# Moving the last exchange's four unchanged blocks, three roundings, the weights' means and one context low part in a gated cross-attention and ternary feed-forward kernel

## Time and profile before

| | |
|---|---|
| median of 3 runs | 649.63 us (649.16 to 651.08) |
| the profiled execution | 650.32 us, its span 648.5 us |
| VectorE, ScalarE, GpSimd busy | 534.8, 422.4, 359.5 us (82%, 65%, 55%) |
| granted TensorE clock | full in all 40 slices |
| chain that ended last | TensorE 75%, VectorE 13%, SyncE's queue 3% |
| DMA | 112.79 MB, mean 174 GB/s |

### The profile page before, as it was taken

One profiled execution on the slowest core, in us unless ns is written; L12 is line 12 of the kernel. 1 busy time (PEld: TensorE's weight loads), 2 busy tenths in 40 slices (PEclk: granted clock), 3 DMA queues, 4 the chain that ended last, 5 costly groups with the idle time before them and its releaser, 6 DMA issues.

```text
span 648.5 us, 9998 instructions
## 1 busy us (share of the span) xinstructions
PE 634.8 (98%) x2968; PEld 394.7 (61%) x2968; DVE 534.8 (82%) x869; ACT 422.4 (65%) x694; POOL 359.5 (55%) x304
## 2 busy tenths in 40 slices
PE   8799999999999999999999999999999999999997
PEld 7565566666666666666666756675656554544553
DVE  5778887789778887878789978897899987998863
ACT  2575686477647765775567766776666632688875
POOL 4712477556635653565367864664457145686651
PEclk9999999999999999999999999999999999999999
DMA  8207985799589948984888789868789881000001
GB/s 292 81 6 202 295 213 118 209 248 258 116 218 271 236 112 244 261 224 108 242 228 223 202 227 249 224 190 205 190 220 254 202 207 45 1 4 31 16 35 49
DMA packets 45208, 112.79 MB, mean 174 GB/s; under 512 B 11888, under 2 KB 15088, under 8 KB 45040
## 3 DMA queue, kind: packets, MB, share of 16 engines
q1 hardware_dynamic: 41648, 102.93, 59.3%
q10 hardware_dynamic: 3456, 9.37, 4.8%
q0 software_dynamic: 64, 0.00, 0.0%
HBM read 45.16 MB, written 2.10 MB: 73 GB/s over the span
## 4 chain that ended last, share of the span: by engine, by line
PE 75%; DVE 13%; SPq 3%; issue 3%; ACT 3%; POOL 1%; DMA 1%; POOLq 0%; DVEq 0%; ACTq 0%
PE ps_s L1462 13%; PE ps_ctx L1494 6%; PE ps_b L1494 6%; PE ps_s L624 5%; PE ps_b L1358 4%; PE ps_b L1413 4%; PE ps_b L1360 3%; PE ps_b L1359 3%; PE ps_b L1432 3%; SPq L1144 3%; DVE small L1884 3%; DVE E L1898 2%; PE ps_b L675 2%; PE ps_b L1490 2%; PE ps_ctx L1490 2%
## 5 line engine op out<-in xcount | busy, mean ns | idle before, releaser
L1260 POOL TENSOR_TENSOR G_lo<-G,g_hi 128x512 fp32r<-128x512 f32 x130 | 167.7, 1303 | 115.5 <-ACT g_hi L1638 115.5
L1696 ACT ACTIVATE E<-ps_s,small 128x1024 f32<-128x1024 f32 x128 | 142.3, 1114 | 133.3 <-DVE small L1884 110.5
L1884 DVE TENSOR_REDUCE small<-ps_s 128x1 f32<-128x1024 f32 x128 | 149.8, 1210 | 37.2 <-PE ps_s L1462 37.0
L1898 DVE STREAM_TRANSPOSE E<-E 128x1024 f32<-128x1024 f32 x124 | 151.9, 1229 | 0.1
L1218 POOL TENSOR_SCALAR E<-E,small 128x1024 f32<-128x1024 f32 x64 | 78.6, 1228 | 107.0 <-DVE small L1890 95.3
L1638 ACT ACTIVATE g_hi<-G 128x512 fp32r<-128x512 f32 x130 | 77.1, 630 | 3.5 <-DVE wq L1914 3.5
L1358 PE MATMUL ps_b<-b_hi,ctx_hi 128*128 128x512 f32 x128 | 66.8, 522 | 0.5 <-DVE ctx_lo L1844 0.5
L1494 PE MATMUL ps_ctx<-G,kv 128*128 128x512 f32 x126 | 64.6, 607 | 0.1
L1494 PE MATMUL ps_b<-G,kv 128*128 128x512 f32 x126 | 63.7, 600 | 0.8 <-DMA G<-E 0.8
L1462 PE MATMUL ps_s<-k_hi,q_hi 64*128 64x512 f32 x256 | 57.3, 444 | 3.6 <-ACT E L1696 3.4
L624 PE MATMUL ps_s<-wq,q12T 128*128 128x512 fp8e4 x256 | 59.8, 379 | 0.1
(11 more groups left out here) (202 smaller groups left out, 1210.7 us busy)
## 6 DMA issues: line engine op xcount, KB each, us to landing
G<-E SPq DMA_DIRECT2D x486, 128.0 KB, 3.0
w_stage<-in_wffn SPq DMA_DIRECT2D x37, 512.0 KB, 5.0
w_stage<-in_wffn ACTq DMA_DIRECT2D x11, 512.0 KB, 4.5
wo_s<-in_woT SPq DMA_DIRECT2D x8, 512.0 KB, 5.3
wq_s<-in_wq SPq DMA_DIRECT2D x7, 512.0 KB, 5.6
wkcq_s<-in_wkcqT SPq DMA_DIRECT2D x7, 384.0 KB, 3.3
out<-x_sb SPq DMA_DIRECT2D x8, 256.0 KB, 2.0
x_sb<-in_x SPq DMA_DIRECT2D x3, 512.0 KB, 7.0
```

What stands on the lines that cost most here:

```text
L1260: nc.gpsimd.tensor_tensor(g_tile(w % 2, i, G_lo), tile, high_part(i).bitcast(F32).rearrange("p (t i q) -> p t i q", t=ST, i=4), ALU.subtra ...
L1696: nc.scalar.activation(out, scores, ACT.Exp, bias=negmax[:, k:k + 1], accum_out=rowsum[:, k:k + 1]).then_inc(exp_done, 1)
L1884: nc.vector.tensor_reduce(negmax[:, k:k + 1], ps_s[:, t % 2, :], AX_X, ALU.max, negate=True).then_inc(max_done, 1)
L1898: nc.vector.transpose(e_tile(w % 2, t), e_tile(w % 2, t)).then_inc(blocks_turned, 1)
```

## The change

- **Exchange of (7,3).** Four of its 16 blocks, those that stay on their partitions, are no longer DMAs: GpSimd copies (0,0) and (2,2) (`keep_pool`), ScalarE (1,1) and (3,3) (`keep_act`), 32 partitions by 1024 elements each. SyncE issues the other twelve; ScalarE issues none. TensorE's first product of (7,3) waits for the twelve and for both engines' copies. GpSimd's copies stand before `ln2_root(0)` and between it and `rms_root(0)`. SyncE's load of g3 waits for the twelve as well.
- **Rounding.** In (5,0), (6,0) and (6,3) the first of the two roundings moves from before the third transpose to between the two maxima of the unit three ahead.
- **Means.** The mean product moves from before pair 4 to behind its first side task "m", VectorE's four operations into the first unit of pair 4 behind the context's low part. The wait on `mean_chain` stays for pair 4 alone.
- **Context's low part.** That of (7,2) moves from the start of (7,3) to step 6 of (7,2), behind the second row tile's quantised rows and before three small steps.

```diff
-SHARED = {(0, 1): 12, (7, 3): 10}
+SHARED = {(0, 1): 12}
+KEPT_POOL, KEPT_ACT = (0, 1), (2, 3)
+KEPT = len(KEPT_POOL) + len(KEPT_ACT)
...
+LATE_ROUND_STEPS, LATE_ROUNDS = (5, 6), ((5, 0), (6, 0), (6, 3))
...
+        CTX_LOW_AT = (2, 6)
...
             sp.wait_ge(exchanged[0], EXCHANGE * UNITS // 2)
+            sp.wait_ge(exchanged[1], exchanged_by(PAIRS - 1, 3))
             sp.dma_start(g3, A["g3"].partition_broadcast(P)).then_inc(ld_g3, 16)
...
                 norm_quant(dve, *ROWQUANT_AT[at])
+            if at == CTX_LOW_AT:
+                ctx_low(dve, PAIRS - 1, 2)
             if at in ROWDEQ_AT:
...
-            move_blocks(sp, w, BLOCKS[0:SHARED.get((p, w), len(BLOCKS))] if isinstance(p, int) else BLOCKS)
+            if isinstance(p, int) and (p, w) == (PAIRS - 1, 3):
+                move_blocks(sp, w, BLOCKS[KEPT:])
+            else:
+                move_blocks(sp, w, BLOCKS[0:SHARED.get((p, w), len(BLOCKS))] if isinstance(p, int) else BLOCKS)
...
             act.wait_ge(blocks_turned, 16 * p + (4 * w + 4))
-            if not (is0(p) and w < 2):
-                act.wait_ge(pv_done, 4 * p + (w - 1))
             move_blocks(act, w, BLOCKS[lo:hi])
+        def kept_block(i):
+            quarter = slice(BLOCKS[i][0] * QUAD, (BLOCKS[i][0] + 1) * QUAD)
+            return G[quarter, 1, BLOCKS[i][0], :, :], E[quarter, 1, BLOCKS[i][0], :, :]
+        def exchanged_by(p, w):
+            kept = 16 * KEPT if isinstance(p, int) and (p, w) == (PAIRS - 1, 3) else 0
+            return 2 * EXCHANGE * p + (EXCHANGE * (w // 2 + 1) - kept)
...
+        def keep_pool(pool, i, of, done):
+            pool.wait_ge(of, done)
+            pool.wait_ge(blocks_turned, 16 * PAIRS)
+            pool.wait_ge(pv_done, UNITS - 2)
+            into, rows = kept_block(KEPT_POOL[i])
+            nc.gpsimd.tensor_copy(into, rows).then_inc(kept_pool, 1)
+            pool.wait_ge(kept_pool, i + 1)
...
+                if last and w == 2:
+                    keep_pool(pool, 0, atanh_pool, 5)
                 if splits(p, w):
                     split_low(pool, p, w, 0)
...
                 if last and w == 2:
+                    keep_pool(pool, 1, ln2_done, 1)
                     rms_root(pool, 0)
...
-                pe.wait_ge(exchanged[w % 2], 2 * EXCHANGE * p + EXCHANGE * (w // 2 + 1))
+                pe.wait_ge(exchanged[w % 2], exchanged_by(p, w))
+                if isinstance(p, int) and (p, w) == (PAIRS - 1, 3):
+                    pe.wait_ge(kept_pool, len(KEPT_POOL))
+                    pe.wait_ge(kept_act, len(KEPT_ACT))
...
+                    if mean and (w, c) == (0, 0):
+                        mean_matmul(pe)
...
-            mean_matmul(pe)
             for p in range(4, 7):
-                pe_pair(pe, p, "mid", mean=True)
+                pe_pair(pe, p, "mid", mean=p == 4)
...
+        def keep_act(act, i):
+            act.wait_ge(blocks_turned, 16 * PAIRS)
+            act.wait_ge(pv_done, UNITS - 2)
+            into, of = kept_block(i)
+            copy_act(into, of).then_inc(kept_act, 1)
...
                     if variant == "last" and (w, c) == (2, 0):
-                        exchange_rest(act, 7, 3, 10, 13)
+                        keep_act(act, KEPT_ACT[0])
                     if variant == "last":
                         ffn_act_early(act, w, c)
                     if variant == "last" and (w, c) == (2, 1):
-                        exchange_rest(act, 7, 3, 13, 16)
+                        keep_act(act, KEPT_ACT[1])
...
+        def weight_means(dve):
+            dve.wait_ge(w_total, 1)
...
+            nc.vector.reciprocal(w_inv, w_eps).then_inc(mean_chain, 1)
...
+                late = isinstance(p, int) and (p, w) in LATE_ROUNDS
                 def rounded(c):
...
-                            if c == ROUND_STEPS[i]:
+                            if c == (LATE_ROUND_STEPS if late else ROUND_STEPS)[i]:
                                 round_half(dve, q, g)
...
-                if w or variant != "first":
+                if (w or variant != "first") and not (variant == "last" and w == 3):
                     ctx_low(dve, *((p, w - 1) if w else (p - 1, 3)))
+                if isinstance(p, int) and (p, w) == (SUM_PAIRS, 0):
+                    weight_means(dve)
...
                 if first:
                     max_tile(dve, *u3, 0)
+                    rounded(5)
                     max_tile(dve, *u3, 1)
```

More of the change, by code:

```diff
@@ L373, in build @@
         exchanged = [sem("exchanged0"), sem("exchanged1")]
+        kept_pool, kept_act = sem("kept_pool"), sem("kept_act")
         first_turned, first_act = (sem(n) for n in ("first_turned", "first_act"))
@@ L1915, in round_half @@
                                     MAGIC, MAGIC, ALU.add, ALU.subtract, saturate=False).then_inc(w_taken, 1)
+        def weight_means(dve):
+            dve.wait_ge(w_total, 1)
+            nc.vector.tensor_reduce(w_mean, mean_psum.rearrange("p (j c) -> p j c", j=3), AX_X, ALU.add).then_inc(mean_chain, 1)
+            dve.wait_ge(mean_chain, 1)
+            nc.vector.tensor_scalar(w_mean, w_mean, -2.0 / (DIM * FF), None, ALU.mult).then_inc(mean_chain, 1)
+            dve.wait_ge(mean_chain, 2)
+            nc.vector.tensor_scalar(w_eps, w_mean, RMS_EPS, None, ALU.add).then_inc(mean_chain, 1)
+            dve.wait_ge(mean_chain, 3)
+            nc.vector.reciprocal(w_inv, w_eps).then_inc(mean_chain, 1)
         def dve_pair(dve, p, variant, mode):
@@ L2094, in _ @@
                 dve_pair(dve, p, "mid", "sum")
[L2096 to L2103, removed]
             for p in range(4, 7):
```

## The result

The changed kernel takes **658.58 us** (median of 4 runs, 657.20 to 659.56) against 650.30 (4 runs, 649.16 to 651.08): 1.0121 times as long, 95% interval 1.0105 to 1.0137. The forecast was 650.7, the range ended at 651.9. Five executions in the experiments took far longer than the others of their kernel (1280.28 us in experiment 3, 1617.96 in 6, 2233.53 and 794.95 in 8, 947.65 in 9) and are left out of the medians and ratios there. The profiled execution of the changed kernel took 658.73 us, span 657.0, 8.5 more than before.

A forecast was written before the change was run, and what follows sets the result against it. TensorE, busy for nearly the whole span, was taken as the bound, so only stalls reaching it or its feeder count. −0.4 + 0.3 + 1.2 + 0.1 − 0.1 = +1.1 us gave 650.7 us, range 648.2 to 651.9.

The forecast's parts named there:

- part 4: SyncE's queue behind the moved rounding of (6,3): exchange of (7,1) begins 1.5 us later, costing +0.1; upper bound +2.1 more.
- The prediction's own sign of being wrong: Start of (7,3): the wait of the first exponential ended by DMA would show the forecast wrong; no size given.
- Slower by more (12%): Exchange of (7,1) lands later than 511.7, taking 4.4 instead of 2.3 us: 652.8 us; chance 12%.
- Part 3: Moved rounding of (6,3): collides with GpSimd's joining of the kv tiles, second maximum late, +1.2 us; bounds 0 and 1.4.
- Part 1: Means at pair 4: TensorE's wait for VectorE to free the bank goes, −0.4 us; gain 0.24 to 0.43.
- Part 2: Rounding in (5,0) and (6,0): b's low part 0.3 us late in (5,0), covered in (6,0); +0.3, bounds 0 and 0.7.
- Part 5: Last exchange: DMA wait of 0.8 us goes, GpSimd's copies delay quantised rows 0.5; −0.1 us, bounds −0.6 and +0.6.
- the rival of 4%: (7,2): VectorE's one-element operations wait for GpSimd's copies, root chain 1.1 instead of 0.5 us late: 651.3 us; chance 4%.

The follow-up runs named there:

- experiment 3: The changed kernel with GpSimd's joining of the first kv tiles one unit earlier, in (6,2) instead of (6,3): 656.74 us, ratio 1.0089.
- experiment 6: The changed kernel with GpSimd's joining one unit earlier and pair 7's two loads ahead of the waiting weight half: 650.41 us against 650.70, ratio 1.0000.
- experiment 8: The changed kernel with no rounding moved and all four kept blocks copied by ScalarE, none by GpSimd: 649.93 us against 650.70, ratio 0.9986.
- experiment 9: The kernel of experiment 8 with VectorE's scaling of the weights' means (128x3) made as three single-column operations: 648.92 us against 650.70, ratio 0.9972.
- experiment 5: The kernel before, with SyncE waiting in (6,3) for the first maximum of (7,2) ahead of its stage load: 657.14 us against 650.70, ratio 1.0103.
- experiment 4: The changed kernel with SyncE's two loads for pair 7 issued ahead of the weight half that waits for the moved rounding: 652.10 us, ratio 1.0029.
- experiment 7: The kernel before, with SyncE starting the exchange of (7,1) only after VectorE's second rounding of (6,3): 651.35 us against 650.56, ratio 1.0016.
- experiment 2: The kernel before with only the rounding of (6,3) moved between the two maxima: 659.11 us, ratio 1.0137.
- experiment 1: The changed kernel with the rounding of (6,3) back in its old place: 650.23 us against 650.31, ratio 0.9996.
- experiment 10: The kernel of experiment 9 with the addition behind the scaling in single columns too: 649.53 us against 650.56, ratio 0.9980.

## Why the prediction was wrong

**The step that failed is part 4**, "+0.1", and its bound. Everything ahead of it in that part held: the load was put at "about 497.5" and came at 497.35, the exchange at 498.8 and came at 498.79. Then the text said that ScalarE's next exponential waits "not for the DMA, with little to spare", and took a landing of 2.3 to 4.4 us from the rows of *another* exchange. The last block took 8.26, since the loads had not only been moved past in the queue: they had been moved out of a stretch in which the DMA engines had room into the one in which they had none. The sum counted SyncE's issues and never its bytes. The prediction's own sign of being wrong, the first exponential of (7,3) ended by a DMA, came: it started at 517.60, behind the last block. Measured, the term is 3.8 us of waiting, 2.0 of the exponential that had waited for the same landing, 1.3 of the lower clock and 0.5 behind it, 7.6 in all (8.69 behind at TensorE's products from 529.30 on, less 1.12). The rival "Slower by more (12%)" had the mechanism and the deadline, 511.7, but the same landing, and so a price of 2.1 where 7.6 was paid; experiments 5, 4 and 7 bear out that the late loads bring it.

**Part 3, +1.2: right.** The rounding took 2.04 us (1.9 expected), with the joining 0.07 us ahead of it (0.13 expected). From 492 us to the scores of (7,0) the changed kernel loses 1.37, experiments 2 and 4, which have the collision, 1.36 and 1.38, and experiments 1, 3, 5, 6 and 7, which don't, 0.01 at most.

**Part 1, −0.4: the sign and nearly the size.** The mean product before pair 4 is gone:

```profile
302.06 0.40 PE L1526 MATMUL ps_b<-G_lo,kv_hi 128*128 128x512 f32 x1
302.30 1.02 PE L1530 MATMUL ps_ctx<-G,kv 128*128 128x512 f32 x2
```

From the scores at 296.75 to those at 304.91 (times of before) the changed kernel gains 0.57, and so does every experiment with the means moved (0.56 or 0.57), while 2, 5 and 7, without it, gain 0.00. The bound was 0.43. From start to start the two products take 0.24 here against 0.86 in the earlier trace rows: 0.62 less, inside the forecast's 0.46 to 0.65. What was mis-sized is the mean product's own issue: put at 0.22, it gave back only 0.05 (0.24 ahead at the first product of pair 4, 0.19 at 304.91). The four operations, costed at 0.7 us if uncovered, take 1.8 with their block, and cost TensorE nothing.

**Part 2, +0.3: the delay in (5,0) was right, "covered" in (6,0) was not.** In (5,0) the low part of b no longer waits, and TensorE does:

```profile
385.53 0.70 PE L1465 MATMUL ps_b<-xn_rows,a_full 128*128 128x512 f32 x1 [0.38 <-DVE b_lo L1918]
```

From 377.50 to 389.15 the changed kernel loses 0.26. But all six experiments without this rounding gain 0.16 to 0.20 on the same step: the profiled execution of before had a slow one. In (6,0), from 442.70 to 454.85, the five kernels with the rounding gain 0.24 to 0.26, and five of the six without it 0.61 to 0.71; the sixth, experiment 10, loses 0.10. The low part of b is the difference: TensorE waits 0.35 us for it in (6,0) in all five kernels with the rounding, not at all in those five without it, and 0.60 and 0.69 in the profiled executions of before and of experiment 10. So "covered" held only against these two slow steps. Against the profiled execution of before the term is 0.0, and against the usual steps the two roundings cost some 0.45 each. Why a step has two lengths without the rounding is open.

**Part 5, −0.1: right**, to 0.2 us. The tail of the changed kernel:

```profile
533.08 1.03 POOL L1290 COPY G<-E 32x1024 f32<-32x1024 f32 x1 [1.47 <-PE ps_b L1530]
534.19 0.73 POOL L548 TENSOR_TENSOR small<-small 128x2 f32<-128x2 f32 x1
534.99 1.03 POOL L1290 COPY G<-E 32x1024 f32<-32x1024 f32 x1
```

```profile
547.82 0.62 PE L644 MATMUL ps_s<-identb,qn 128*128 128x128 bf16 x8 [1.34 <-DVE qn L945]
```

No wait for DMA at the start of (7,3) is left, and the wait for the quantised rows has grown, as forecast: the weight load of the earlier trace rows, which waited 0.85 us, waits 2.17 now, and the product behind it 1.34. GpSimd's copies took 1.03 us, not 1.2; in experiment 1, whose times there compare directly, the two roots start at 525.47 and 527.43, 0.3 and 0.4 late instead of 0.5, and the turning of the quantised rows at 539.10 is 0.2 late, not 0.5. VectorE's one-element operations beside the second copy take 0.45 and 0.21 us for two, as they did before without it: the rival of 4% did not come. From 529.30 to the gate products at 550.72 (8.69, then 8.42 behind) the changed kernel gains 0.27.

By steps, then: −0.57 + 0.26 − 0.25 + 1.37 + 7.57 − 0.27 = 8.1 us, of a span that grew by 8.5; nearly all of the remaining 0.4 was there at 296.75, ahead of every place that the change touches. Without part 4 it is +0.5 where the forecast had +1.0: nearly all of the error is one term. That the rest comes so near is partly luck of the trace compared with: against the usual steps of part 2 it would be +1.4.

## What to carry to other kernels

When a step is moved, follow the semaphore that it sets to the loads that wait for it, add up the bytes they carry, and look at the DMA share of the stretch that they leave and the one that they enter; a price from another transfer's landing time holds only at the same load. Whatever needs no wait goes ahead of what does in a DMA queue: here one swap in the queue took back over 6 of 8 us. And a wait that ends late costs TensorE more than itself, because the engines behind it had waited for the same thing and the clock had fallen.

## What the runs showed of the hardware that was not expected

- **The DMA engines' rate in this mix.** In the six stretches of the changed kernel from 500 to 524 us, with a DMA share near 1, they move 211 to 262 GB/s, block exchange within SBUF, weight loads and broadcast gains together. Other mixtures moved more at such a share: 280 in 492 to 496 us before, 312 in 500 to 504 us in experiment 6. So a share near 1 is no fixed rate. The Trainium skill (DMA: Bandwidth & Descriptors, the section on where 436 GB/s comes from) puts the ceiling of the SBUF ports at 435 GB/s; no stretch here comes near it. By that ceiling alone 4.3 million bytes take some 10 us, an estimate from that page, against 18 at the measured rate, which decides.
- **The form of a small operation.** Beside GpSimd, a scaling of 128x3 took 1.21 and 0.90 us instead of 0.2, three of 128x1 took 0.28 in all. The Trainium skill (VectorE: DVE Perf Modes, on mode 2×_2P) has the condition for the two-port mode: a single input and the output in SBUF, with the outermost dimension that isn't one even, or odd and equal on both sides. Read so, three columns fulfil it and a single one has no such dimension; the traces of experiments 9 and 10 agree. One row does not fit: the addition of 128x3 at 306.46 took 0.20 us with GpSimd's scaling beside it from 306.39, and the same pair stands in every trace with that order, experiments 1, 3, 4, 6 and 8. Why it passed is not shown.
- **The clock.** In the changed kernel the granted clock was 1.00 in 512 to 516 us, where TensorE was idle for 2.1 of 4 us, 0.69 in 516 to 520 and 0.50 in 520 to 524 us, when it was at work again. Experiments 2, 3 and 5 show the same fall (0.50, 0.65 and 0.63 in 516 to 520), experiments 4 and 6, without the wait, 1.00.
